# Another order of the stages in a kernel's begin and end lists, on all four engines

## What is computed

```python
x = x + L0(x, cond)   # per entry a weight of rank 30: U = cond @ W_dec + b_dec, weight = U @ V
x = x + L1(x, cond)   # x * styles, matmul with weight, * dcoefs, + bias, clip to +-256
x = x + L2(x, cond)   # relu(x @ w_down) @ w_up + x, both weights scaled per entry
# L3: six variants of the row, concatenated, then an MLP and a layer norm
h = ln(ln(x, pw_g[ids], pw_b[ids]), cp_g[comp], cp_b[comp])
t = ln(x, tm_g[..]); s = ln(x, ms_g[..])
m, n, r = x + mlp_ln(memory), x + mlp_ln(noise), x + mlp_ln(resource)
cat = concat(w0*h, w1*t, w2*m, w3*n, w4*r, w5*s)      # w = softmax(aw)
out = ln(silu(cat @ int_W1 + b1) @ int_W2 + b2)
```

## Time and profile before

| | |
|---|---|
| median of 3 runs | 523.67 us |
| the profiled execution, its own time | 521.21 us |
| its span, first to last instruction | 519.4 us |
| TensorE busy | 486.3 us, 94% |
| VectorE, ScalarE, GpSimd busy | 78%, 65%, 75% |
| mean granted TensorE clock | 0.994 |
| begin lists on TensorE | 0 to 96.68 us |
| ten chunks of the loop | 96.68 to 374.87 us |
| end lists on TensorE | 374.87 us to the end |

### The profile page before, as it was taken

The page is one execution under the profiler, slowest core; times in us unless marked ns, Lnnn a source line. Parts: engine busy times, 40 slices in busy tenths (PEclk is TensorE's granted clock), DMA queues, the critical chain, the costliest instruction groups (busy, mean ns, idle before and its releaser), DMA issues.

```text
span 519.4 us, 9425 instructions
## 1 busy us (share of the span) xinstructions
PE 486.3 (94%) x3198; PEld 354.2 (68%) x3198; DVE 405.8 (78%) x696; ACT 336.3 (65%) x638; POOL 391.0 (75%) x367
## 2 busy tenths in 40 slices
PE   2987887999999999999999999999999999998993
PEld 2953644767677776768686867677776768687682
DVE  2958876868788788888787878788787888886863
ACT  4573667456767676766777776767676767656832
POOL 6468799889878879697978787788779793787321
PEclk9999999999999999999999999999999999999997
...
GB/s 299 247 304 208 203 20 124 163 73 135 83 127 81 77 171 56 191 24 223 0 229 17 205 43 173 74 136 112 106 142 63 175 47 90 49 21 145 40 2 81
DMA packets 34989, 61.78 MB, mean 119 GB/s; under 512 B 5017, under 2 KB 17413, under 8 KB 34580
## 3 DMA queue, kind: packets, MB, share of 16 engines
...
## 4 chain that ended last, share of the span: by engine, by line
PE 79%; POOL 6%; DVE 5%; DMA 4%; issue 3%; ACT 2%; SPq 0%; DVEq 0%; POOLq 0%; ACTq 0%
PE ps_c L902 11%; PE ps_c L904 11%; PE ps_c L903 10%; PE ps_d L948 9%; PE ps_d L962 5%; PE ps_a L976 5%; PE ps_b L902 3%; PE ps_b L903 3%; PE ps_b L904 3%; PE ps_b L935 2%; PE ps_a L988 2%; DMA set_wdec<-in_nets_rows 2%; PE ps_a L994 2%; PE ps_b L994 2%; DMA set_wdec<-in_W_dec 1%
## 5 line engine op out<-in xcount | busy, mean ns | idle before, releaser
L1507 POOL DMA_INDIRECT pw_rows<-in_pw,gidx x64 | 65.0, 1016 | 17.9 <-issue 17.4
L948 PE MATMUL ps_d<-xm_t,l_w 128*128 128x512 f32 x128 | 59.0, 603 | 2.2 <-POOL xm_t L1516 2.2
L1209 ACT ACTIVATE h<-h,nb_h,rstd_h 128x256 f32<-128x256 f32 x64 | 33.3, 591 | 33.1 <-POOL nb_h L1531 33.0
L1240 ACT ACTIVATE tm_t_h<-ps_a 128x1024 fp32r<-128x1024 f32 x16 | 16.4, 1026 | 45.6 <-DVE ps_a L1413 45.6
L1516 POOL TENSOR_TENSOR xm_t<-x_t,style 128x1024 f32<-128x1024 f32 x16 | 30.5, 1905 | 20.2 <-DVE x_t L1345 20.1
L948 PEld LDWEIGHTS ps_d<-xm_t,l_w 128*128 128x128 f32 x128 | 23.1, 190 | 26.8 <-issue 24.2
L1546 POOL TENSOR_TENSOR h<-xhat,pw_rows 128x1024 f32<-128x1024 f32 x16 | 38.0, 2378 | 4.1 <-ACT xhat L1209 4.1
L1565 POOL TENSOR_TENSOR w_up<-up_rep,ugub 128x1024 f32<-128x1024 f32 x16 | 38.0, 2372 | 2.2 <-issue 2.0
L1551 POOL TENSOR_TENSOR h<-h,pw_rows 128x1024 f32<-128x1024 f32 x16 | 38.3, 2394 | 1.3
L1567 POOL TENSOR_TENSOR w_up<-w_up,ugub 128x1024 f32<-128x1024 f32 x16 | 38.1, 2382 | 1.3
L902 PE MATMUL ps_b<-w_h,act_t_l 128*128 128x256 f32 x128 | 37.7, 294 | 0.4 <-DVE act_t_l L1450 0.4
...
## 6 DMA issues: line engine op xcount, KB each, us to landing
...
pw_rows<-in_pw,gidx POOLq DMA_INDIRECT x64, 3.7
...
```

Of the source, the lines that this page charges most:

```text
L948: m = eng.matmul(ps_l1[:, o, :], l1_w[:, k, o * P:(o + 1) * P], xm_t[:, k, :], start=k == 0, stop=k == KB - 1)
L1209: m = eng.activation(out[:, j, :], src[:, j, :], ACT.Identity, bias=nb[k][:, j:j + 1], scale=rstd[k][:, j:j + 1])
L1507: eng.indirect_dma_start(pw_rows[c.ring][:, j, :], None, t["pw"], bass.IndirectOffsetOnAxis(ap=gidx[c.ring][:, j:j + 1], axis=0)).then_inc ...
```

## The change

The begin and end lists of TensorE, ScalarE, VectorE and GpSimd hold the same stages with the same chunks as before, in another order. The loop's `order` lists and SyncE's lists are the same, and so is every stage. Two lines of the diff:

```diff
-                             (act_u, 0), (act_exp, 0), (act_ug, 0), (act_th1, 0), (act_th2, 0), (act_sqrt, 0),
-                             (act_hid, 0), (act_w1scale, 0), (act_w2high, 0), (act_u, 1), (act_th1, 1),
...
+                             (act_u, 0), (act_dg, 0), (act_gidx, 1), (act_ug, 0), (act_th1, 0), (act_exp, 0),
+                             (act_th2, 0), (act_hid, 0), (act_sqrt, 0), (act_w1scale, 0), (act_u, 1),
```

More of the change, by code:

```diff
@@ L1659, in _ @@
-                             (act_hh, 0), (act_tmh, 0), (act_relu, 2), (act_x3h, 1), (act_msh, 0), (act_xht, 1),
-                             (act_hnorm, 1), (act_silu, 0), (act_silh, 0), (act_x3, 2), (act_th1, 4), (act_hh, 1),
-                             (act_xnorm, 2), (act_tmh, 1), (act_relu, 3), (act_gidx, 4), (act_ysquare, 0),
-                             (act_msh, 1), (act_xht, 2), (act_x3h, 2), (act_th2, 4), (act_onehot, 2)],
+                             (act_ubwrite, 0), (act_turn, 7), (act_turn, 9), (act_turn, 10), (act_turn, 12),
@@ new lines, in _ @@
+                             (act_x3h, 0), (act_xnorm, 0), (act_th1, 2), (act_xht, 0), (act_relu, 1),
+                             (act_th2, 2), (act_hnorm, 0), (act_rowwrite, 0), (act_th1, 3), (act_onehot, 1),
+                             (act_shift, 0), (act_gidx, 3), (act_x3, 1), (act_hh, 0), (act_xnorm, 1),
+                             (act_tmh, 0), (act_x3h, 1), (act_xht, 1), (act_relu, 2), (act_msh, 0),
+                             (act_th2, 3), (act_hnorm, 1), (act_silu, 0), (act_gidx, 4), (act_th1, 4),
@@ L1663, in _ @@
+                             (act_silh, 0), (act_x3, 2), (act_onehot, 2), (act_th2, 4), (act_xnorm, 2),
+                             (act_hh, 1), (act_tmh, 1), (act_relu, 3), (act_ysquare, 0), (act_msh, 1),
+                             (act_xht, 2), (act_x3h, 2)],
                       order=[(act_u, 1), (act_hnorm, 4), (act_silu, 5), (act_gidx, 1), (act_silh, 5),
```

149 lines of the change are left out of this document (73 added, 76 removed).

## The result

The changed kernel took 528.30 us (median of 4 runs, 527.09 to 528.76), the kernel before 523.43 us beside it (4 runs): ratio 1.0085, 95% interval 1.0062 to 1.0108. It is slower by more than 0.3%, where no change was forecast, and lies above the range of 521.3 to 526.0. Four executions of this study, of three kernels, took 785 to 1703 us; none of them is used. The profiled execution is the one of 528.76 us; its span is 526.9 us against 519.4, so the two profiles lie 7.5 us apart and the medians 4.9.

What follows compares the result with a forecast made beforehand. TensorE, busy 94% of the span with a full loop, was taken as the bound. Begin part -0.8 and end part +0.9 gave +0.1 on the profiled 521.2, so 521.3, and a median of 523.8; range 521.3 to 526.0.

Steps and rivals of the forecast that it cites:

- the begin part with the first trip: Up to and into the loop: -0.7 at `pe_xht(1)`, -0.2 in the first trip, +0.1 for the gather, -0.8 in all.
- the end part: After the loop: 2.1 us late at `pe_up(15)`, partly won back later, +0.9 in all.
- The decode: Start of the begin part: the last sum ends 28.5 instead of 27.7, +0.8.
- the style's square: Begin part: taken as 0.95 us, standing ahead of the last `v_decode`; the faster rival (0.27) allowed 0.45.
- The third table load: Ahead of `act_silu(0)`: its 1.28 us disappear in that stage's wait of 2.23 for TensorE, cost 0.
- The early gather: `g_gather(0)` moves from 40.3 to 33.4, beside the row load: 0.1 late taken, up to 0.8 kept.
- the slower rival: Chance 0.21: q0 and q1 take turns evenly, `v_mostat` up to 3.3 later, 525.9 (0.13); or a longer end (0.08).
- The eight waits: TensorE's waits of 0.6 to 1.4 us each before the loop, after the first load, most on `v_x2add`.
- the softmax, behind it, 0.6: Begin part: softmax takes 0.6 behind the reciprocal, so `act_w1scale` starts at 40.85 instead of 37.03.
- I would be wrong altogether if the loop's first trips lost time (GpSimd enters it with one gather, 5 us, still to issue): Loop entry: named as a sign that the forecast fails altogether; no size or chance given for the loss.
- The walk: Both lists followed from wait to wait with stage durations and latencies from the trace; summed to +0.1, 521.3 on the profile.
- 476.21 becomes 477.25, +1.05.: End part: the chain from `pe_x3r(15)` to `pe_tm(14)`, now bound by ScalarE, ends 1.05 later.

Runs made afterwards that it cites:

- the kernel with the two begin repairs: Changed kernel's begin lists with softmax early and GpSimd's last begin stages as before, end lists of the kernel before: 521.94 us against 522.39, ratio 0.9994.
- `pe_t(3)` behind, old end lists: Begin lists with early softmax and GpSimd's old tail, old end lists, `pe_t(3)` behind `pe_cp(0)` and `pe_x3r(1)`: 522.11 us against 522.31 before, ratio 0.9997.
- all three faults repaired: Changed kernel with softmax early, GpSimd's last begin stages as before and `g_hadd(14)` ahead of `g_gather(15)`: 524.03 us against 521.81 before, ratio 1.0029.
- the new end lists alone: Begin lists of the kernel before with the changed kernel's end lists: 524.39 us, ratio 1.0026 to the kernel before.
- The old lists with the late root: Kernel before with square root behind hidden layer and softmax last: 528.59 us, ratio 1.0119; with `g_style(0)` also ahead of `g_dcoef`: 522.61 us, ratio 1.0005.
- GpSimd's tail alone: Changed kernel with only GpSimd's last begin stages in their old order: 525.47 us against 522.39 for the kernel before, ratio 1.0050.
- the move of `pe_t(3)`: Changed kernel with early softmax, GpSimd's old tail, `g_hadd(14)` back, plus `pe_t(3)` behind `pe_cp(0)` and `pe_x3r(1)`: 522.97 us against 522.31 before, ratio 1.0004.

## Why the prediction was wrong, step by step

**In the terms of the sum.** The forecast was +0.1 us on the profile. For the begin part with the first trip it had -0.8, and the profiles have +1.5; for the second trip nothing, and they have +4.2; for the end part +0.9, and they have +1.8. Each of the three has a step of its own that failed, and a part of the first two is the granted clock, for which the sum had no term.

**What held.** The decode ends at 28.50 (predicted 28.5), `pe_x1(0)` starts at 33.69 (33.65). The agreement is partly luck: with the same lists the decode ends from 27.7 to 28.6 in other profiles, and the style's square took 0.41 us, not 0.95. The third table load lies mostly in the wait for TensorE (its matmuls end at 110.96, the load at 111.53), and no wait of TensorE follows. The early gather: row load some 0.5 late (0.1 taken, 0.8 kept as bound), and the delay of up to 3.3 us of the slower rival did not come. Its second victim, `ugub`, which landed at 50.0, was in no step, and cost nothing either. Without falls, `pe_tm(0)`, `pe_dn(2)` and `pe_xht(1)` start at 91.08, 91.40 and 95.99 (predicted 91.2, 91.55, 95.95) in the kernel with the two begin repairs. In the end part `pe_up(15)` is 1.97 later than before, counted from `pe_xht(11)` (predicted 2.1), with a wait of 0.49 of `pe_dn(15)` (predicted 0.5). Here the sum is better than its terms. As written they add up to 1.95, not 2.1. `pe_w1_ms(12)` and `pe_up(15)` come 0.2 and 0.1 later behind the stage in front of them, where 0.3 and 0.5 were forecast, and `pe_l1(14)` has a wait of 0.24 for `xm_t` that is in no step. (The eight waits that the prediction counts ahead of the loop are eleven; its sum does not use the count.)

**The step that failed first: "the softmax, behind it, 0.6".** It took 2.43, 2.09 of it for one operation of 128x6 numbers; `act_w1scale` began at 42.48 instead of 40.85, `v_l1mul(0)` at 47.63 instead of 46.1, and `u_ch`, behind `act_w1scale` on ScalarE, kept `pe_t(1)` waiting 1.78. How much of the begin part this is can be read at `pe_t(3)`, counted from `pe_x1(0)`: 49.5 us in the changed kernel, 48.7 in the one with `g_hadd(14)` moved (the same begin lists, no fall up to there), 46.9 to 47.4 in three with the early softmax and no fall up to there. So the late softmax costs 1.4 to 1.9 us there and the two falls 0.8. In the times it does not show: where only the softmax differs, on one chip, the medians lie 0.4 us apart. That GpSimd holds the operation is shown by moving GpSimd's stages alone: 2.09 became 0.86 in the set-up, 2.98 became 1.22 in the end part. It could have been seen in the kernel before: the 0.95 of the style's square in the earlier trace rows is such a case, beside this operation of GpSimd, which had 0.7 us left.

```profile
28.10 1.12 POOL L825 TENSOR_TENSOR set_b2f<-set_b2f 3x256 f32<-3x256 f32 x1
```

In twelve profiles with the new begin lists the square starts ahead of that operation, and takes 0.41 or 0.42. In the thirteenth (`pe_t(3)` behind, old end lists) it starts 0.07 us behind it and takes 0.92.

**"I would be wrong altogether if the loop's first trips lost time (GpSimd enters it with one gather, 5 us, still to issue)."** This was named and not priced, and it is the largest item: 2.48 us of waiting in the second trip, and in this execution the fall behind it. The cause is the order at the end of GpSimd's list: `g_style(3)` stands ahead of `g_res(1)`, so that GpSimd waits 1.75 us for `v_x1add(3)` with 2.36 us of work behind it that was ready, and `g_gather(3)` stands last. The two were put back together, so how much each is worth is not shown. The walk stopped at `pe_xht(1)`, as if TensorE's time there were all that the begin lists hand on. GpSimd's time is handed on too; with 226 us of work in 278 it catches up slowly. And `pe_l1(c)` waits for `v_hprod(c-2)`, since it overwrites the bank that `v_hprod` reads: this wait was in no step. Restoring the tail removed it.

**"476.21 becomes 477.25, +1.05."** It became +1.94, because `pe_x3r(15)` waited 0.94 for `v_x3sum(15)`, behind the stretched `v_x3low(14)`. With `g_hadd(14)` moved the end part is 0.76 longer than before, against the predicted 0.9.

**What the sum left out.** With all three faults repaired the walk gives about +0.4 (the end's 0.66 in that kernel, less the 0.26 left at `pe_xht(2)`, which is itself within the spread of the begin places). Measured were 2.2 by the medians and 1.5 by the ratio, and the interval reaches down to 0.2, so that a rest is likely and not certain. It goes with the clock: 0.988 instead of 0.992 is about one fall more per run, and a fall costs up to 1.7. Every version with the new begin lists had a lower mean clock (0.985 to 0.991) than the kernel before, the new end lists alone had not. (The old lists with the late root had 0.983 and 0.990.) A lower clock is not always a longer time, though: the kernel with the two begin repairs and the old end lists had 0.990 and the time of the kernel before, and with GpSimd's tail alone the four runs at 0.990 (524.5 to 524.9) were faster than the five at 0.991 to 0.994 (525.3 to 526.5). The falls in these profiles stand inside a wait of TensorE or right behind one: those at 34 to 35 us behind one of 0.4, the others behind waits of 1.2 to 4.6. But a wait does not always bring a fall: `pe_t(3)` with its wait of 1.7 to 2.0 us has one behind it in seven profiles of twelve, `pe_l1(4)` with 2.5 in three of six. And the kernel before, whose clocks went down to 0.981, must have falls in other runs. That an order with longer single waits is hit more often fits the mean clocks and the move of `pe_t(3)`; it is argued from them and not shown, since the interval of no single move settles it. What makes a fall come in one execution and not in the next stays open.

The clock may also explain why medians (4.9) and profiles (7.5) differ: the profile of before was an execution without falls ahead of the last microseconds, 2.2 us below its median.
